# AdaLN attention and feed-forward block: turning the keys by DMA instead of on TensorE, and moving three steps of each attention block into the next

## What is computed

```python
h = layernorm(x) * (1 + ca) + sa
q = silu(h @ wq);  k = sigmoid(h @ wk);  v = h @ wv;  f = 1 - k
# per head, with the sign of (f - 0.5) carried along in the decay:
S = S * f[..., None] + k[..., None] * v[..., None, :]     # state, 128 x 128
o = einsum('bhk,bhkv->bhv', q * scale, S)
out = layernorm(o * sigmoid(h @ wg1 @ wg2)) * norm_w
x = x + ga * (out @ wo)
x = x + gb * ffn(layernorm(x) * (1 + cb) + sb)
```

## Time and profile before

| | |
|---|---|
| time, median of 3 runs | 1739.95 us (1739.4 to 1740.9) |
| time of the profiled execution | 1739.65 us |
| its span, first to last instruction | 1737.9 us |
| PE busy | 1716.6 us, 99% of the span |
| DVE busy | 1542.1 us, 89% |
| ACT busy | 1011.3 us, 58% |
| POOL busy | 408.0 us, 23% |
| granted TensorE clock, mean | 0.998 of full |

### The profile page before, as it was taken

The page is one execution under the profiler, slowest core; times in us unless marked ns, Lnnn a source line. Parts: engine busy times, 40 slices in busy tenths (PEclk is TensorE's granted clock), DMA queues, the critical chain, the costliest instruction groups (busy, mean ns, idle before and its releaser), DMA issues.

```text
span 1737.9 us, 45170 instructions
## 1 busy us (share of the span) xinstructions
PE 1716.6 (99%) x18493; PEld 1540.0 (89%) x18493; DVE 1542.1 (89%) x3483; ACT 1011.3 (58%) x1645; POOL 408.0 (23%) x359
## 2 busy tenths in 40 slices
PE   9999999999999999999999999998999999999999
PEld 7889889998999988998999999987888888888888
DVE  7898888999999999999999998998888888888885
ACT  4454545556665566556665566554466666666664
POOL 1000101101111011101111011102455555555552
PEclk9999999999999999999999999999999999999999
DMA  6122113322223222322223223320333333343331
GB/s 243 41 62 72 38 38 78 71 62 50 62 56 81 51 53 62 95 63 50 62 57 80 51 50 62 70 91 25 110 86 109 86 98 101 82 110 86 97 92 43
DMA packets 217526, 129.29 MB, mean 74 GB/s; under 512 B 175572, under 2 KB 177384, under 8 KB 217320
## 3 DMA queue, kind: packets, MB, share of 16 engines
q1 hardware_dynamic: 217304, 126.39, 28.7%
q10 hardware_dynamic: 16, 0.00, 0.0%
HBM read 48.77 MB, written 34.60 MB: 48 GB/s over the span
## 4 chain that ended last, share of the span: by engine, by line
PE 92%; DVE 6%; issue 1%; ACT 0%; POOL 0%; DVEq 0%; ACTq 0%; POOLq 0%
PE bank L1457 65%; PE lvl L1457 9%; PE bank L1564 3%; PE bank L1563 3%; PE bank L1571 3%; PE lvl L1532 3%; PE bank L1555 2%; PE lvl L1515 1%; PE lvl L1550 1%; PE lvl L1544 1%; PE bank L1465 0%; DVE xn L139 0%; PE bank L1791 0%; DVE xk L1102 0%; DVE ln_st L117 0%
## 5 line engine op out<-in xcount | busy, mean ns | idle before, releaser
L133 POOL TENSOR_TENSOR ln_rs<-ln_ve,mhalf 128x2 f32<-128x2 f32 x64 | 82.0, 1281 | 577.8 <-DVE ln_ve L128 577.5
L449 POOL COPY og_halves<-og 128x1024 uint16<-128x1024 uint16 x60 | 66.1, 1102 | 428.5 <-DVE og L1058 428.5
L1457 PE MATMUL bank<-hT_hi,wq_hi 128*128 128x256 f32 x512 | 148.2, 289 | 1.5 <-DVE hT_lo L861 1.2
L1457 PE MATMUL bank<-xk_hi,fk_hi 128*128 128x256 f32 x512 | 145.8, 285 | 2.6 <-DVE xk_lo L1115 2.6
L1457 PE MATMUL bank<-hT_hi,wk_hi 128*128 128x256 f32 x512 | 148.2, 289 | 0.0
L1457 PE MATMUL bank<-xk_hi,fk_lo 128*128 128x256 f32 x512 | 145.6, 284 | 0.0
L1457 PE MATMUL bank<-xk_lo,fk_hi 128*128 128x256 f32 x512 | 145.5, 284 | 0.0
L1457 PE MATMUL bank<-hT_hi,wq_lo 128*128 128x256 f32 x512 | 144.9, 283 | 0.0
L1457 PE MATMUL bank<-hT_lo,wk_hi 128*128 128x256 f32 x512 | 144.9, 283 | 0.0
L1457 PE MATMUL bank<-hT_lo,wq_hi 128*128 128x256 f32 x512 | 144.8, 283 | 0.0
L1457 PE MATMUL bank<-hT_hi,wk_lo 128*128 128x256 f32 x512 | 144.7, 283 | 0.0
(11 more groups left out here) (240 smaller groups left out, 5827.0 us busy)
## 6 DMA issues: line engine op xcount, KB each, us to landing
xs<-in_L_attn_x SPq DMA_DIRECT2D x32, 512.0 KB, 3.8
x_scratch<-xs SPq DMA_DIRECT2D x32, 512.0 KB, 3.0
xs<-x_scratch SPq DMA_DIRECT2D x32, 512.0 KB, 3.6
out<-xs SPq DMA_DIRECT2D x31, 512.0 KB, 2.8
mod_raw<-in_L_wmod SPq DMA_DIRECT2D x6, 1024.0 KB, 7.0
raw_q<-in_L_attn_wq SPq DMA_DIRECT2D x2, 512.0 KB, 4.7
raw_k<-in_L_attn_wk SPq DMA_DIRECT2D x1, 1024.0 KB, 5.7
raw_v<-in_L_attn_wv SPq DMA_DIRECT2D x1, 1024.0 KB, 6.8
```

The lines of the kernel that those rows point to most:

```text
L133: pool.tensor_tensor(out=ln["rs"][:, :], in0=ln["ve"][:, :], in1=mhalf[:, :], op=ALU.pow).then_inc(ln["rstd"], 1)
L449: pool.tensor_copy(halves[:, ch, :].rearrange("p (two e) -> p two e", two=2), og[n % 2][:, ch, :].bitcast(U16).rearrange("p (e two) -> p t ...
L1457: last = pe.matmul(dst, lhs(a, s), rhs(b, s), start=(t == 0), stop=(t == len(terms) - 1))
```

## The change

It holds for blocks n with `keys_by_dma(n)`, which are 6 to 29 (in the code: `cur` where block n is one, `prev` where block n - 1 is one).

- PE no longer turns the keys. POOL splits them into 16-bit halves in Kt (`keys_split`), SP turns the halves (`turn_k`) into `k_halves_turned`, which lies on the room of `xn_halves`, and ACT joins them into Kt in the next block (`keys_joined`), between its two `q_gate`.
- The state products, `state_mid`, `state_end`, `output(n, 1)` and `gated(n, 1)` of block n move into block n + 1: on PE behind both q halves (then `pair_product(n+1, 1)`, then the output), on DVE around `joint(n+1, 1)`. The state products go to banks 4 and 5 and the output's second half to bank 0.
- On DVE, `ln_var` and `apply_next` come earlier, `diagonal` and `first_merge` come before `gated(n, 0)`; `gated_stats(n-1, 1)`, `gated_var(n-1)` and `joined_low` come later. On ACT, `h_join` comes before the gates, `spread_diagonal` before the second half of k and f.
- `pair_product(n+1, 0)` stays where it was in time, as the last of block n. The load of the feed-forward weight r is issued later in its block.

Helpers and buffers:

```diff
+def keys_by_dma(n):
+    return n >= 0 and n + 2 < NB and by_dma(n + 2)
...
+        k_halvesT = at("k_halves_turned", [P, NC, 2 * H, P], 198, U16)
         xn_halves = at("xn_halves", [P, NC, 2 * E], 198, U16)
```

On SP:

```diff
+                def turn_k(n, ch):
+                    sp.wait_ge(k_halved, kept_dma(n, ch))
+                    sp.dma_start_transpose(k_halvesT[:, ch, :, :],
+                                           Kt[:, ch, :, :].rearrange("p h d -> p (h d)").bitcast(U16)).then_inc(k_turned[ch], 16)
...
+                    late = n < LAST and keys_by_dma(n - 1)
-                    if 0 < n < LAST:
+                    if 0 < n < LAST and not late:
                         turn_og(n - 1, 1)
...
+                    if late:
+                        turn_og(n - 1, 1)
...
                         for ch in range(NC):
                             turn_rows(n + 2, ch)
+                    if keys_by_dma(n):
+                        for ch in range(chunks_kept(n)):
+                            turn_k(n, ch)
                     if n < LAST - 1:
                         turn_og(n, 0)
```

On POOL:

```diff
+                def keys_split(n, par, ch):
+                    pool.wait_ge(level, NU * (n + 1))
+                    if n > 0:
+                        pool.wait_ge(mm["ds"], kept_before(n))
+                    pool.wait_ge(xn_joined, NC * (dma_before(n + 2) + 1))
+                    pool.tensor_copy(Kt[:, ch, :, :].rearrange("p h d -> p (h d)").bitcast(U16).rearrange("p (two h t) -> p two h t", two=2, h=H),
+                             K[par][:, :, :].bitcast(U16).rearrange("p (h c) (t two) -> p c two h t", c=NC, two=2)[:, ch]).then_inc(k_halved, 1)
...
                     ln_rstd(pool, ln, mhalf, n + 2)
+                    if keys_by_dma(n):
+                        for ch in range(chunks_kept(n)):
+                            keys_split(n, n % 2, ch)
                     if n < LAST - 1:
                         og_split(n, 0)
```

On ACT:

```diff
+                def keys_joined(n, ch):
+                    act.wait_ge(k_turned[ch], 16 * columns_dma(n, ch))
+                    act.copy(Kt[:, ch, :, :].rearrange("p h d -> p (h d)").bitcast(U16).rearrange("p (h d two) -> p two h d", h=H, two=2),
+                             k_halvesT[:, ch, :, :].rearrange("p (two h) d -> p two h d", two=2)).then_inc(kt_sb, 1)
...
                     q_gate(n + 1, 1 - par, 1)
+                    if prev:
+                        for ch in range(chunks_kept(n - 1)):
+                            keys_joined(n - 1, ch)
                     q_gate(n + 1, 1 - par, 0)
...
-                    for ch in range(chunks_kept(n)):
-                        keys_turned(n, ch)
+                    if cur:
+                        if not prev:
+                            for ch in range(NC):
+                                xn_split(n + 2, ch)
+                        for ch in range(NC):
+                            h_join(n + 2, ch)
                     for ch in range(NC):
                         gate(n + 1, 1 - par, ch)
```

On DVE:

```diff
                     q_silu(n + 1, 1 - par, 1)
+                    if prev:
+                        state_mid(n - 1)
+                        if not closing(n - 1):
+                            state_end(n - 1)
                     joint(n, 1)
                     q_silu(n + 1, 1 - par, 0)
+                    if prev:
+                        gated(n - 1, 1)
                     pair_update(n, par, 1)
                     pair_merge(n, par, 1)
+                    if prev:
+                        gated_stats(n - 1, 1)
+                        gated_var(n - 1)
+                        joined_low(n - 1, 0)
+                    if dma:
+                        ln_stats(dve, ln, n + 2)
+                        ln_var(dve, ln, n + 2)
                     f_signed(n + 1, 1 - par, 0, spare)
                     if dma:
-                        ln_stats(dve, ln, n + 2)
+                        apply_next(n + 2)
...
                     variants(n + 1, 1 - par, 0)
+                    if cur:
+                        diagonal(n + 1, 1 - par)
+                        first_merge(n + 1, 1 - par)
                     gated(n, 0)
-                    state_mid(n)
-                    if not closing(n):
-                        state_end(n)
                     gated_stats(n, 0)
                     if n + 2 < NB:
                         h_high(n + 2)
```

On PE:

```diff
                     rows_of("q", 0, 2, "q")
+                    if prev:
+                        for ch in range(chunks_kept(n - 1)):
+                            state_step(n - 1, 1 - par, ch)
+                        pair_product(n, par, 1)
+                        pe.wait_ge(s_mid, n)
+                        output(n - 1, 1 - par, 1)
...
                     pe.wait_ge(gate_sb, 2 * (n + 1))
+                    if prev:
+                        pe.wait_ge(og_sb, 2 * n)
                     v_rows(0)
...
-                    for ch in range(chunks_kept(n)):
-                        turn_keys(n, par, ch)
+                    if not cur:
+                        for ch in range(chunks_kept(n)):
+                            turn_keys(n, par, ch)
...
+                    if cur:
+                        pair_product(n + 1, 1 - par, 0)
```

More of the change, by code:

```diff
@@ L180, in kept, with kept_by, kept_pe, kept_dma @@
     return 2 * n + ch + 1 - (n > BPB - 1)
+def kept_by(turned_so, n, ch):
+    return sum(chunks_kept(j) for j in range(n) if turned_so(j)) + ch + 1
+def kept_pe(n, ch):
+    return kept_by(lambda j: not keys_by_dma(j), n, ch)
+def kept_dma(n, ch):
+    return kept_by(keys_by_dma, n, ch)
+def columns_dma(n, ch):
+    return sum(keys_by_dma(j) and ch < chunks_kept(j) for j in range(n + 1))
 def kept_before(n):
@@ L699, in attention_body @@
                         act.copy(W["o"][0][:, :, :], raw_o2[:, :, :]).then_inc(w_hi["o"], 1)
-                    if n > 0:
+                    prev, cur = keys_by_dma(n - 1), keys_by_dma(n)
+                    if n > 0 and not prev:
                         og_join(n - 1, 0)
@@ L725, in attention_body @@
                         gate_copy(n + 1, bank[1])
+                    if prev:
+                        og_join(n - 1, 1)
+                        joined_high(n - 1, 1)
                     v_copy(n + 1, 1 - par, 0)
-                    spread_diagonal(n)
+                    if prev and cur:
+                        for ch in range(NC):
+                            xn_split(n + 2, ch)
+                    if not prev:
+                        spread_diagonal(n)
                     merge_32(n, par)
@@ L736, in attention_body @@
                         gate_copy(0, bank[3])
-                    if by_dma(n + 2) and n + 2 < NB:
+                    if cur:
+                        if not prev:
+                            for ch in range(NC):
+                                xn_split(n + 2, ch)
                         for ch in range(NC):
-                            xn_split(n + 2, ch)
-                    for ch in range(chunks_kept(n)):
-                        keys_turned(n, ch)
+                            h_join(n + 2, ch)
+                    else:
+                        for ch in range(chunks_kept(n)):
+                            keys_turned(n, ch)
                     for ch in range(NC):
                         gate(n + 1, 1 - par, ch)
[L744 to L750, removed]
+                    if cur:
+                        h_scaled(n + 2)
+                    elif n + 2 < NB:
+                        h_affine(n + 2)
                     if n == 0:
@@ L1198, in attention_body @@
                     par = n % 2
+                    prev, cur = keys_by_dma(n - 1), keys_by_dma(n)
                     joint(n, 0)
-                    if n > 0:
+                    if n > 0 and not prev:
                         gated_stats(n - 1, 1)
-                    if n > 0:
                         gated_var(n - 1)
-                    else:
+                    if n == 0:
                         centre_wo()
@@ L1271, in attention_body @@
                         h_high(n + 2)
-                    diagonal(n + 1, 1 - par)
-                    first_merge(n + 1, 1 - par)
+                    if not cur:
+                        diagonal(n + 1, 1 - par)
+                        first_merge(n + 1, 1 - par)
                     if n == LAST - 1:
@@ L1281, in attention_body @@
                         weight_low("r", [3])
-                    gated(n, 1)
+                    if not cur:
+                        gated(n, 1)
                 def crossing():
@@ L1559, in output @@
                     from_state = ch > 0 or not fresh(n)
+                    dst = bank[0] if ch and keys_by_dma(n) else bank[2]
                     for h in range(H):
@@ L1590, in attention_body @@
                     par = n % 2
+                    prev, cur = keys_by_dma(n - 1), keys_by_dma(n)
                     if n == 0:
                         pe.wait_ge(mean_copied, 1)
-                    pair_product(n, par, 0)
```

(2 more changed lines are left out.)

86 lines of the change are left out of this document (55 added, 31 removed).

## The result

The changed kernel takes 1749.39 us (median of 4 runs, 1747.01 to 1752.61), the kernel before 1740.43 us in the same comparison (1739.4 to 1741.08). The ratio is 1.0054, 95% interval 1.0042 to 1.0066: 9 us slower. The profiled execution has a span of 1747.7 us where before had 1737.9, so these two traces differ by 9.8 us.

A forecast was written before the change was run, and what follows sets the result against it. It took PE to bound the kernel, with DVE close behind. 20 ordinary blocks by 0.2, +4, and edges +2.5 gave +6 us on 1739.65: 1746 us, range 1724 to 1756.

The forecast's parts named there:

- the mechanism in the ordinary block: POOL copies delay DVE, next q products wait for `h_lo`: period 35.85 us against 35.64; chance 0.40.
- The output's time: PE's input for `gated(n, 0)` ready at t = 31.40, moved from 28.62 by +3.58 and -0.80.
- The key copies hold `variants`: POOL's two `keys_split` copies delay DVE's `variants` by 0.25 and 0.86, so `gated(n, 0)` starts at 32.0.
- The cast is held: DVE's cast of `h_high` waits for POOL's `og_split(n, 0)`, going 0.14 before the copy's end.
- The tail: From the start of `gated(n, 0)` to the next block's q products: 3.85 us, including 0.26 for PE's start.
- Copies that fall where they don't hurt: Rival: POOL's key copies come later than `variants` or lose the race; period 35.25, 1732 us; chance 0.22.
- The prediction's rule that the first to issue wins: DVE copies, casts in two-port mode and two-SBUF-input instructions share an exclusive lock with GpSimd, taken by whoever issues first.
- Block 6: First changed block gives work away to the next: -3.1 us.
- Blocks 15 to 17 and 30: 15 and 16 lose their head start, +1; 17 has four more subtractions, +1; 30 takes the moved work, +3.6.
- The first feed-forward blocks: Feed-forward part after the attention blocks: no change, 0.
- What I said is hidden: `keys_joined`, 1.36 each, runs from 3.8 to 6.5 behind `q_gate`; turned keys have 8 us, 3.2 to landing each.
- +6.5: Whole kernel: 20 ordinary blocks by 0.2, +4, and edge blocks +2.5.

The follow-up runs named there:

- The run with the memset: Changed kernel with POOL's key copies replaced by memsets writing the same 1024 16-bit elements of Kt per chunk, reading nothing: 1730.92 us, ratio 0.995.
- both edits: Changed kernel with two POOL waits: `keys_split` waits for `variants(n+1, 0)`, `og_split(n, 0)` for `h_lo`: 1726.66 us, ratio to before 0.9919.
- the three runs named under the last experiment: Changed kernel, each alone: without key copies, 1730.91 us; key copies replaced by memset, 1730.92 us; `og_split(n, 0)` kept back until `h_lo`, 1742.32 us.
- the run with the gates first: Changed kernel with `keys_split` and `og_split(n, 0)` both kept back, plus ACT's gates ahead of `h_join` in block 6: 1725.96 us, ratio 0.9917.

## Why the prediction was right, and where its terms were off

The direction, the mechanism in the ordinary block and the time (1746 forecast, 1749.39 measured, within 1724 to 1756) held. That the total came out so near is in part luck. The steady blocks, on which the mechanism was worked out, give +0.7 of the 9.8 us and not +3.6; the rest comes from the blocks at the edges, whose prices were estimates, and 2.3 of it (1.4 in block 6 and 0.9 in the feed-forward part, an estimate from the traces below) from stretches at the lower clock, for which the forecast had no term. Point by point:

- **The output's time.** Input of `gated(n, 0)` at t = 31.40: the runs in which nothing holds DVE start it at 31.29 to 31.30. Right to 0.1.
- **The key copies hold `variants`.** Predicted 0.25 + 0.86 = 1.11 and `gated(n, 0)` at 32.0. Measured 1.03 and 32.04, from copies at t = 28.32 and 29.58 (predicted 28.5 and 29.5). The first run without the copies shows it as the cause.
- **A write-only POOL instruction.** The prediction didn't tell reading from writing. The run with the memset does, for a product with two SBUF inputs.
- **The cast is held.** Predicted from a 4-column copy. Shown by the run that moves `og_split`: 1.00 becomes 0.68.
- **The tail.** Predicted 3.85 from `gated(n, 0)` to the next block, measured 35.72 - 32.04 = 3.68. The term that was mis-sized is PE's start after `hT_lo`: 0.26 taken from the earlier trace rows, while L944 ends at 772.62 + 1.23 = 773.85 and PE starts at 773.91, 0.06 after. That is 0.20 less, against 0.07 more in the terms ahead of it, and it made 35.72 where I had 35.85: +0.08 a block in place of +0.2.
- **Copies that fall where they don't hurt.** I held this for one rival out of five for all blocks. It came true in blocks 11 and 24, -1.0 us. That POOL, once it is second, waits through three products is not in the prediction. Each of the two possible orders is in the trace; the copies ask 0.9 us later in 11 and 24 than in the ordinary block. The prediction's rule that the first to issue wins doesn't tell the two apart by their starts. (Its "in every block" for L968 is too much; 29 of 30, a few lines on, is right.)
- **Blocks 12 to 15** have one more DVE instruction than the others, which I had not looked for: `gate_wo2`, L1267, here the line's own view (shortest, median, longest in ns).

```profile
L1267 DVE TENSOR_TENSOR raw_o<-raw_o,gab x4: 681/682/685, 501.8 to 610.3; 128x512 f32<-128x512 f32 x4
```

  Before, DVE had 1.73 of slack ahead of `gated(n, 0)` and it cost nothing. With DVE on the cycle it is 0.6 to 0.9 in blocks 13 and 14. In block 12 the second `h_join` came late and POOL was the one held, which hid it. In the run with both edits these blocks still take 35.04 to 35.14.
- **Block 6**, the largest miss (-3.1 predicted, -0.5 measured). I counted the work that PE gives away, 3.1, and not when the next input can be ready: `h_lo` is set at t = 33.8 (304.52 + 1.23, from a block start at 271.97), since `h_join` waits for its DMA. That alone leaves 33.8, or -1.8, as in the three runs named under the last experiment. The change also puts `h_join` ahead of the gates. ACT, then PE:

```profile
298.24 2.55 ACT L592 COPY hF<-xn_halves_turned 128x1024 uint16<-128x1024 uint16 x2 [2.29 <-DMA xn_halves_turned<-xn_halves]
300.66 1.07 ACT L651 ACTIVATE og<-bank 128x512 f32<-128x512 f32 x2
...
299.27 0.39 PE L1662 MATMUL bank<-V,A 128*128 128x128 f32 x2
301.82 0.76 PE L1554 MATMUL bank<-wo_hi,ogT_hi 128*128 128x512 f32 x1 [2.17 <-issue]
302.38 0.63 PE L1554 MATMUL bank<-wo_lo,ogT_hi 128*128 128x512 f32 x1
```

  PE waits for both gates ahead of `wo_rows` and stands 2.17 us. In the run with the gates first, `wo_rows` starts 1.70 after the output's first product; here it is 4.11 (297.71 to 301.82). Behind the idle stretch the granted clock is, in this execution, at its lower level, 1.2 GHz, for 3.4 us, and a product starts every 0.43 us in place of 0.23. That is the step from 33.8 to 35.15; other runs have the same idle stretch and keep the full clock:

```profile
301.50:305.00 3.50, 3.18 (x8) 2.53 (x9) 1.25 (x2) 2.18 (x5) 2.44 (x3) 0.53 0.52 102
```

- **Blocks 15 to 17 and 30**: +2.7 and +4.2 for +2 and +3.6. The head start that 15 and 16 had is gone as I wrote (1.0 and 0.5), and block 17 gives the other 1.1. **The first feed-forward blocks**, which the change doesn't touch, are 0.9 longer: the clock is at the lower level for 6.8 us there instead of 3.4.

```profile
1189.00:1196.20 7.20, 5.62 (x38) 4.03 (x41) 3.58 (x9) 3.28 (x8) 0.00 (x0) 0.53 0.20 74
```

- **What I said is hidden**, is: `keys_joined` runs from t = 3.67, no wait on Kt shows in the waits of PE, and the turned keys land in 3.3 us. The state products took 1.88 and the output 1.8 where I had 1.71 and 1.87.

In short: the 3.3 us between +6.5 and +9.8 are what two errors of opposite sign leave, 2.9 too much in the ordinary blocks with 11, 24 and 27 (predicted 3.6, measured 0.7), and 6.2 too little in all others.

## What to carry to other kernels

A copy on GpSimd that reads SBUF has a second price, the stretch of VectorE work with two SBUF inputs, or the cast, that it stands beside; look for pairs of equal VectorE instructions of which one is long, and give such copies an explicit wait that puts them beside PSUM work or behind the critical step. When you delay one, follow what is queued behind it: here each of two waits gave a third of a microsecond a block and both together a full one. Where a step takes an engine from slack to none, look through all blocks for instructions that this slack had hidden, not only through the ordinary one. And before a gain in one stretch is put down to an edit, look at the same stretch in runs that don't have the edit: in block 6 that took 1.4 of 1.75 us away.

## What the runs showed of the hardware

- Beside a POOL copy of 1.04 us, a DVE product of 0.42 takes up to 1.26 and ends 0.25 to 0.28 after the copy; a cast of 0.68 takes 1.00 (or 1.47, when the copy starts late) and ends 0.55 after it. Beside a POOL write of 0.95 us the product is unchanged; no run has the cast beside one.
- Two POOL copies in a row (766.50 and 767.76, block 19) let one waiting DVE product through between them. A POOL copy that came in while DVE had a row of products waited for all three of them, 2.0 us for one of 1.04 (block 24).
- The spread between executions of one kernel goes for the most part with the mean granted clock: with both edits, 1723.23 us at 0.999 and 1726.51 to 1727.05 at 0.997; with block 6 changed too, 1722.97 at 0.999 and 1725.79 to 1727.04 at 0.997. The changed kernel has an exception, 1752.61 at 0.997 against 1749.86 at 0.996. One stretch at the lower level more or less is as large as a small edit: 1.4 us in block 6, behind the same idle stretch of 2.2 us that leaves the clock at its full level in five other runs. What decides whether it comes in an execution stays open.
